# Two decoder layers on eight elements: attention calls in another order, the start regrouped, the routing in smaller steps

## What is computed

```python
# layer 0 (norm before), layer 1 (norm after); ctx is the second input
h = ln1(x); x = x + attn(h, h, causal=True)                # first call  (c = 0)
h = ln2(x); x = x + attn(h, ctx, causal=False)             # second call (c = 1)
h = ln3(x); x = x + relu(h @ w1 + b1) @ w2 + b2            # feed-forward, FFN
x = LN1(x + attn(x, x, causal=True))                       # third call  (c = 2)
x = LN2(x + attn(x, ctx, causal=False))                    # fourth call (c = 3)
x = LN3(x + moe(x))    # router: 2 of 8 experts for each row, gelu, all float32
```

## Time and profile before

| | |
|---|---|
| median of 3 runs | 1236.32 us (1233.37 to 1236.89) |
| profiled execution: its own time, its span | 1233.35 us, 1231.6 us |
| PE, DVE, ACT, POOL busy | 89%, 67%, 59%, 42% of the span |
| mean granted TensorE clock | 0.954 of full speed |
| first `max` matmul of call 0; last `shift` (call 31); first expert matmul | 27.69 us; 844.10 us; 912.42 us |

### The profile page before, as it was taken

How to read it: one execution, slowest core, us unless ns; L and a number is a source line. 1 busy time by engine, 2 the same in 40 slices (tenths; PEclk the granted TensorE clock), 3 DMA queues, 4 the chain that set the end, 5 groups by cost and what they waited for, 6 DMA issues and landing times. The chain is left out here.

```text
span 1231.6 us, 27064 instructions
## 1 busy us (share of the span) xinstructions
PE 1099.5 (89%) x8981; PEld 907.1 (74%) x8981; DVE 821.4 (67%) x2495; ACT 729.9 (59%) x1537; POOL 513.8 (42%) x732
## 2 busy tenths in 40 slices
PE   8688889999999999998899988887879999999960
PEld 7466667768877788876667766555669999999960
DVE  2677878775555555546767777764348888888856
ACT  4345555665555454545566666544338988988842
POOL 4354555331122213434667245442241544544544
PEclk9799999999999999999999999987889999999985
DMA  7575747664344433434746644540656777787764
GB/s 167 90 118 130 120 73 100 84 120 59 43 59 61 52 53 53 87 53 54 160 76 95 88 71 87 95 81 27 228 201 181 250 227 230 240 246 232 237 177 145
DMA packets 110312, 152.35 MB, mean 124 GB/s; under 512 B 23040, under 2 KB 94976, under 8 KB 103424
## 3 DMA queue, kind: packets, MB, share of 16 engines
q1 hardware_dynamic: 101712, 140.21, 51.7%
q0 software_dynamic: 8352, 10.80, 4.5%
q10 hardware_dynamic: 144, 0.02, 0.0%
HBM read 78.39 MB, written 21.62 MB: 81 GB/s over the span
## 5 line engine op out<-in xcount | busy, mean ns | idle before, releaser
L875 ACT ACTIVATE probs<-s 128x384 f32<-128x384 f32 (+1 forms) x512 | 265.5, 541 | 194.4 <-PE s L683 174.3
L946 DVE TENSOR_REDUCE neg_max<-s 128x2 f32<-128x512 f32 x256 | 169.7, 689 | 95.4 <-PE s L658 89.2
L683 PE MATMUL s<-q_stack,k_stack 98*128 98x256 bf16 (+1 forms) x1024 | 176.9, 262 | 14.4 <-ACT probs L875 13.3
L541 POOL TENSOR_SCALAR_AFFINE_SELECT probs<-probs 128x256 f32<-128x256 f32 x256 | 102.3, 409 | 179.7 <-ACT probs L875 179.6
L943 DVE CUSTOM_DVE_ANT_0 s<-s,mask_qk 128x256 f32<-128x256 f32 x256 | 114.2, 446 | 86.0 <-PE s L655 78.0
L683 PEld LDWEIGHTS s<-q_stack,k_stack 98*128 98x128 bf16 x1024 | 90.7, 99 | 40.2 <-ACT probs L875 24.6
L702 PE MATMUL pv<-probs,v 128*32 128x256 f32 (+1 forms) x2048 | 116.1, 369 | 4.0 <-POOL probs L541 3.9
L658 PE MATMUL s<-k_stack,q_stack 96*128 96x256 bf16 x512 | 98.2, 276 | 12.8 <-DVE neg_max L946 11.2
L1303 PE MATMUL moe<-rows_hi,e_w_hi 128*128 128x256 f32 x368 | 104.8, 285 | 3.7 <-DVE rows_lo L1414 2.3
L1303 PE MATMUL moe<-e_w_hi,e_hidden_hi 128*128 128x256 f32 x368 | 104.6, 284 | 0.0
L604 PE MATMUL work<-hT,w_qk 128*128 128x256 f32 x384 | 94.9, 391 | 10.8 <-ACTq L797 10.8
(11 more groups left out here) (195 smaller groups left out, 2651.4 us busy)
## 6 DMA issues: line engine op xcount, KB each, us to landing
w<-in_expert_w SPq DMA_DIRECT2D x26, 1024.0 KB, 5.2
k_stack<-k_part SPq DMA_DIRECT2D x192, 128.0 KB, 4.3
q_stack<-q_part SPq DMA_DIRECT2D x192, 128.0 KB
e_w<-in_expert_w SPq DMA_DIRECT2D x24, 1024.0 KB
rows<-slots_x SPq DMA_DIRECT2D x25, 256.0 KB
slots_x<-filler SPq DMA_DIRECT2D x8, 518.0 KB
cT<-in_context SPq DMA_DIRECT2D x16, 256.0 KB, 4.5
e_b<-in_expert_b SPq DMA_DIRECT2D x24, 128.0 KB
```

Of the source, the lines that this page charges most:

```text
L541: pool.affine_select(out=blocks, in_=blocks, compare_op=ALU.is_ge, fill=0.0, base=0, pattern=[[0, TILES], [1, P]], channel_multiplier=-1). ...
L683: last = pe.matmul(dst[:, kt * S:kt * S + S - q0], k[:, kt * P:(kt + 1) * P], q[:, q0:S], start=True, stop=True)
L875: act.activation(probs[hd][:, 0:width], s2[hd % 2][:, 0:width], ACT.Exp, scale=SCALE).then_inc(probs_ready, 1)
L946: dve.tensor_reduce(neg_max[:, :, hd], src[:].rearrange("p (t s) -> p t s", t=TILES), AX_X, ALU.max, negate=True).then_inc(s1_free, 1)
```

## The change

The calls get a new order: `CALL_OF_SLOT` names the call of each of the 32 slots, lanes in order within each kind. Slots 0 to 7 are the eight first calls and 8 to 14 seven second ones, as before; then come third call 0, second call 7, third calls 1 to 3, fourth 0, third 4, fourth 1, third 5 and 6, fourth 2, third 7, fourth 3 to 7. All that was numbered `c * B + lane` is numbered by slot. The weights of q and k for the third and fourth calls are loaded as soon as the last projection that used their buffer is done, those of v and o as before.

Beside it: (1) call 1 has its norm, `T`, `k`, `q` and `v` ahead of the maxima of call 0, the unused transposes come behind its `v` and are 40 instead of 80, and for calls 0 and 1 ACT, not SP, issues the six DMAs of `q_stack`. (2) DVE's `choose` ends after the maxima of the logits, and the rest of it is a step `pick`; `give_slots` ends where the ranks' bank is free, and the rest is a step `place`. (3) Some due times move by 0.1 to 1.3 units. ACT's copy of the transposed rows (`T`) comes one exponential earlier in each beat, DVE's `wo` one head later, POOL's `bias` one mask earlier, ACT's `scale` of a final norm one exponential later.

```diff
-LAG = {"scalar": {"T": 0.1, "q": 1.4, "k": 1.7, "v": 2.0, "out_T": 0.1, "up": 1.4, "head": 0.6, "shift": 0.5, "final_T": 0.5, "out": 1.4, "scale": 2.4},
-       "vector": {"max": 0.6, "q": 2.2, "k": 1.9, "shift": 2.8, "wo": 1.6, "down": 0.4, "turn": 0.7, "ln": 0, "apply": 3.6, "router": 0.6, "rank": 1.0},
-       "gpsimd": {"mask": 0.6, "bias": 0.2, "ln": 0, "gain": 3.3, "q": 3.7, "k": 2.9, "scatter": 0},
-       "sync": {"q": 5.2, "k": 5.8, "shift": 0.5, "store": 0.2, "fetch": 0.3, "context": 0.1}}
-AT = {"shares": (68.5, 71.5, 74.0, 77.0), "fill": 79.0, "ln": -7.4, "T": -1.9, "q": 0.4, "k": -0.9, "v": 6.4, "bias": 11.7, "context": 8.3, "max": 14.8, "shift": 28.3, "head": 32.8, "weigh0": 43.7,
-      "weigh1": 50.0, "turn": 52.5, "out_T": 55.0, "wo": 56.5, "ffn_ln": 59.5, "ffn_T": 62.7, "ffn_bias": 67.4, "up": (68.0, 73.3, 75.1, 76.7),
-      "down": (79.0, 81.5), "final_ln": 59.3, "final_T": 64.7, "store": 63.1, "router": 65.5, "rank": 67.7, "scatter": 85.5, "post_ln": -15.3}
+LAG = {"scalar": {"T": 0, "q": 1.4, "k": 1.7, "v": 1.9, "out_T": 0.1, "up": 1.4, "head": 0.6, "shift": 0.5, "final_T": 0.5, "out": 1.4, "scale": 2.4},
+       "vector": {"max": 0.5, "q": 2.2, "k": 1.9, "shift": 2.8, "wo": 1.6, "down": 0.4, "turn": 0.7, "ln": 0, "apply": 3.6, "router": 0.6, "rank": 1.0, "pick": 0.6,
+                  "place": 0.6},
+       "gpsimd": {"mask": 0.6, "bias": 0.2, "ln": 0, "gain": 3.4, "q": 3.7, "k": 2.9, "scatter": 0},
+       "sync": {"q": 5.2, "k": 5.8, "shift": 0.5, "store": 0.3, "fetch": 2.8, "context": 0}}
+AT = {"later": 0.0, "pick": 65.9, "place": 68.60000000000001, "shares": (68.5, 71.5, 74.0, 77.0), "fill": 79.0, "ln": -7.5, "T": -1.9, "q": 0.4, "k": -0.8,
+      "v": 6.4, "bias": 10.4, "context": 8.3, "max": 14.8, "shift": 28.3, "head": 32.8, "weigh0": 43.7, "weigh1": 50.0, "turn": 52.5, "out_T": 55.0,
+      "wo": 56.5, "ffn_ln": 59.5, "ffn_T": 62.8, "ffn_bias": 67.4, "up": (68.0, 73.3, 75.1, 76.7), "down": (79.0, 81.5), "final_ln": 59.9, "final_T": 64.7,
+      "store": 63.1, "router": 65.5, "rank": 67.8, "scatter": 85.5, "post_ln": -15.3}
+SECOND = {"ln": -3.0, "T": 1.0, "q": 8.0, "k": 7.0, "v": 9.0}
+ACT_STACKS = 2
+CALL_OF_SLOT = "00000000111111121222323223233333"
+ORDER = [(int(c), CALL_OF_SLOT[:n].count(c)) for n, c in enumerate(CALL_OF_SLOT)]
 def plan_call(n):
-    c, lane = divmod(n, B)
+    c, lane = ORDER[n]
...
+    if n == 1:
+        steps = [(SECOND["ln" if kind == "apply" else kind] - SLOT if kind in SECOND or kind == "apply" else at, kind, lane, arg) for at, kind, lane, arg in steps]
...
                 else:
-                    _, c = what
-                    if c >= 2:
-                        sp.wait_ge(work_full, filled("wo", B - 1, c - 2))
-                    load_qk(c)
-                    load_vo(c)
+                    part, c = what
+                    if part in ("w", "qk"):
+                        if c >= 2:
+                            sp.wait_ge(work_full, max(filled("q", B - 1, c - 2), filled("k", B - 1, c - 2)))
+                        load_qk(c)
+                    if part in ("w", "vo"):
+                        if c >= 2:
+                            sp.wait_ge(work_full, filled("wo", B - 1, c - 2))
+                        load_vo(c)
...
             def stack_q(lane, c):
-                n = c * B + lane
+                n = CALL[c, lane]
+                if n < ACT_STACKS:
+                    return
...
-                if lane == 0 and c == 0:
-                    idle(2 * WARM)
+                if lane == 1 and c == 0:
+                    idle(WARM)
...
                     last.then_inc(ready, 1)
+                    if kind == "q" and n < ACT_STACKS:
+                        stack_q(n)
                 return step
+            def stack_q(n):
+                for i in range(PARTS):
+                    act.wait_ge(q_part_ready[i], n + 1)
+                    for block, p in enumerate(Q_PART_OF_ROWS):
+                        if p == i:
+                            act.dma_start(q_stack[n][block * DK:(block + 1) * DK], q_part[i][:]).then_inc(q_stacked[n], 16)
...
                 for i in range(TILES):
                     dve.max(ordered[:, i, :], logits[:, i, :])
+
+            def pick(lane, stage):
                 dve.drain()
+                ordered = top[:]
...
                 dve.sem_inc(freed("rank", lane, stage), 1)
+
+            def place(lane, stage):
                 dve.tensor_tensor(slot_chosen[:], chosen[:], slot_e[:].unsqueeze(1).to_broadcast([P, TOP, TILES, E]), ALU.mult)
```

More of the change, by code:

```diff
@@ L89, in plan_call @@
         steps += plan_norm(AT["post_ln" if c in POST else "ln"], lane, c)
-    if not CAUSAL[c] and c // 2 * B + lane + CONTEXTS < 2 * B:
+    if not CAUSAL[c] and CONTEXT[c, lane] + CONTEXTS < 2 * B:
         steps += [(AT["context"], "context", lane, c)]
@@ L97, in plan_call @@
     if c == 1:
-        steps += plan_norm(AT["ffn_ln"], lane, FFN) + [(AT["ffn_T"], "T", lane, FFN), (AT["ffn_bias"], "bias", lane, FFN)]
-        steps += [(at, kind, lane, j) for kind in ("up", "down") for j, at in enumerate(AT[kind])]
+        later = FFN_LATER[lane]
+        steps += plan_norm(AT["ffn_ln"] + later, lane, FFN) + [(AT["ffn_T"] + later, "T", lane, FFN), (AT["ffn_bias"] + later, "bias", lane, FFN)]
+        steps += [(at + later, kind, lane, j) for kind in ("up", "down") for j, at in enumerate(AT[kind])]
@@ L100, in plan_call @@
     elif c == CALLS - 1:
-        steps += plan_norm(AT["final_ln"], lane, FINAL) + [(AT[kind], kind, lane, FINAL) for kind in ("final_T", "store", "router", "rank", "scatter")]
-        steps += [(at, "share", lane, i) for i, at in enumerate(AT["shares"])]
+        steps += plan_norm(AT["final_ln"], lane, FINAL) + [(AT["store"], "store", lane, FINAL)]
+        later = AT["later"] * (B - 1 - lane)
+        steps += [(AT[kind] + later, kind, lane, FINAL) for kind in ("final_T", "router", "pick", "rank", "place", "scatter")]
@@ L103, in plan_call @@
+        steps += [(at + later, "share", lane, i) for i, at in enumerate(AT["shares"])]
         if lane in (B - 3, B - 2):
-            steps += [(AT["fill"], "fill", lane, FINAL)]
+            steps += [(AT["fill"] + later, "fill", lane, FINAL)]
+    if n == 1:
+        steps = [(SECOND["ln" if kind == "apply" else kind] - SLOT if kind in SECOND or kind == "apply" else at, kind, lane, arg) for at, kind, lane, arg in steps]
     return [(n * SLOT + at, kind, lane, arg) for at, kind, lane, arg in steps]
@@ L108, in plan_fetches, with at @@
 def plan_fetches():
+    def at(c, lane):
+        return SLOT * CALL[c, lane]
     steps = [(1.5, "fetch", 0, "rows")]
[L111 to L113 removed]
+    steps += [(at(0, lane) - SLOT * 3 + 3.0, "fetch", lane, "x") for lane in range(3, B)]
@@ new lines, in plan_fetches @@
+    steps += [(at(1, 0) - SLOT * FETCH["w"] + 2.0, "fetch", 0, ("w", 1)), (at(1, 0) - SLOT * FETCH["ffn"] + 2.0, "fetch", 0, "ffn"),
+              (at(1, 0) - SLOT * FETCH["contexts"] + 2.0, "fetch", 0, "contexts"), (at(1, 0) - SLOT + 2.0, "fetch", 0, "router")]
+    steps += [(at(c - 2, B - 1) + after, "fetch", 0, (what, c)) for c in (2, 3) for what, after in (("qk", FETCH["qk"]), ("vo", FETCH["vo"]))]
+    steps += [(at(1, B - 1) + SLOT * FETCH["expert"] + max(FFN_LATER[B - 1], 0), "fetch", 0, "expert")]
@@ L346, in run, with norm_before @@
                 step[kind](lane, arg)
+        def norm_before(lane, stage):
+            same = [(other, s) for _, kind, other, s in STEPS if kind == "ln" and use(s) == use(stage)]
+            at = same.index((lane, stage))
+            return same[at - 1] if at and by_three(*same[at - 1]) else None
         def wait_norm(engine, lane, stage):
@@ L897, in norm @@
                 k = use(stage)
-                if lane > 0 and by_three(lane - 1, stage):
-                    dve.wait_ge(rstd_ready, nth("ln", lane - 1, stage))
+                other = norm_before(lane, stage)
+                if other:
+                    dve.wait_ge(rstd_ready, nth("ln", *other))
                 for i in range(TILES):
@@ L1073, in _ @@
             run({"ln": others(norm), "apply": others(apply_norm), "q": rest("q", q_part[0], q_rest, bq, q_part_ready[0], q_rest_ready), "k": rest("k", k_part[0], k_rest, bk, k_part_ready[0], k_rest_ready),
-                 "max": row_max, "shift": rest_of_shift, "turn": normalise, "wo": attended, "down": fed_forward, "router": choose, "rank": give_slots, "share": share}, LAG["vector"])
+                 "max": row_max, "shift": rest_of_shift, "turn": normalise, "wo": attended, "down": fed_forward, "router": choose, "pick": pick, "rank": give_slots, "place": place, "share": share}, LAG["vector"])
             tiles_of_experts()
```

54 lines of the change are left out of this document (31 added, 23 removed).

## The result

The changed kernel takes 1226.77 us (median of 6 runs, 1225.24 to 1227.65), the kernel before 1233.48 (6 runs on the same chip, 1230.85 to 1236.89): a ratio of 0.995, 95% interval 0.9931 to 0.9969. It is faster, by 7 us where 20 were forecast.

What follows compares the result with a forecast made beforehand. PE, busy 89% of the span, was taken as the bound. Terms 0 - 13 - 3 - 4 + 0 = -20 gave 1213 us from the profiled 1233.35 and 1216 from the median 1236.32; predicted 1215, range 1201 to 1230.

Steps and rivals of the forecast that it cites:

- The order of calls, 0: Mixing third and fourth calls among second and third adds no PE work and gains 0 us, ends -6 and +6.
- The final beats, -13: Five `shift`-to-`shift` windows with final steps: routing cut in two on DVE frees PE's waits, 137.55 to 124.5 us.
- second payment: After PE's wait for a maximum in final beats, slow matmuls at low clock cost 1.65 us or more again.
- Rival B: DVE's rank, `turn` and `place` block is only moved; final beats keep most of their 27 us: -9, 1226 us; chance 0.17.
- The start, -4: Call 0's maxima run without call 1's work among them; its `shift` comes near 43.1 instead of 47.04 us: -4.
- ACT's copy one exponential earlier, -3: PE's projections wait less for ACT's copy of T, about 0.4 us in each of nine causal beats: -3 us.
- POOL jamming (C): Beats 21 to 26: causal masks wait on POOL behind gains or scatter, stopping PE; +10, 1245 us; chance 0.05.
- a paying mixture (A): All parts work, final beats fall to PE's work and causal beats give their room: -32, 1203 us; chance 0.17.
- The first expert matmul: Sign in the changed profile that the forecast is right: the first expert matmul comes near 892 us.

Runs made afterwards that it cites:

- the start alone: Kernel before, old order, with only the new start (call 1 early, ACT issuing q stacks, 40 unused transposes, other fetch lags): 1228.12 us, ratio 0.996.
- the changed kernel's second profile: Profile from the control group that ran the changed kernel again unaltered: 1227.3 us (12 runs), ratio 0.9971.
- the last set: Second set of the changed kernel with place, final_T, router and pick later: 1224.4 us; the same without the new start: 1225.17 us.
- the first experiment: Changed kernel with the calls in the order of before, new start, due times and smaller routing steps kept: 1225.01 us, ratio 0.9936.
- the small steps alone: Kernel before, old order, with only the routing cut in two (pick with rank behind maximum 7, place behind turn): 1228.5 us, ratio 0.9979.

## Why the forecast was half right

*The order of calls, 0: right,* shown by three pairs of kernels that differ in nothing else (-2, -2 and -4.5 us for the old order, none beyond its interval). All three have the small steps; beside the routing in one piece the new order has no such pair, and there it seems to cost some 5 us (1.0 with it, 0.996 for the start alone with the old one, two kernels that differ in some due times too). That it adds no PE work held. What the forecast missed is that two things about cancel in it: in the three pairs of profiles the finals are 5 to 7 us shorter among causal calls, and FFN and plain beats are 6 to 11 us longer. Two of these costs were seen: the 1.69 us for `h_ffn`, and beat 28, a plain beat of 23.44 us, in which the last lane's norm lies on DVE (PE waits 1.83 us for a maximum at 774.37).

*The final beats, -13: this is the step that failed;* it measured -4.77. Of the miss of 13.5 us (forecast -20, measured -6.50), 8.2 lie in the final beats, 5.0 in FFN and plain beats (2.17 + 2.85), 0.5 in what comes ahead of beat 11 (the start and ACT's copy), and 0.3 go the other way behind them. The -4.77 is not the mechanism of the forecast either: PE's idle time in these beats, which was to fall, went from 19.15 to 19.21 us. The step that failed is the wait that the sum put at nothing with the words "PE next asks for maximum 8, which is behind rank, `turn` and `place`, but PE has `v` (1.7 us) to do first". The block lasts 3.6 us, so 1.7 us of `v` cover half of it. The forecast had both numbers, gave the block its own rival at 0.17, and still did not set one against the other in its sum. In beats 22, 24, 27 and 29 PE waits 1.58, 1.57, 1.42 and 0.61 us for maxima, 5.2 in all. That place is what made the block too long is shown by the run that moves it alone: these waits go, and 4.4 us of the four beats with them, against the changed kernel's second profile.

*Waits that weren't named.* The final transposes on PE wait 4.2 us for POOL's gain in the same four beats. POOL now does that gain beside the masks of a causal call, which fourth calls don't have. The forecast named the gain for what it does to masks and to DVE's cast, and not for PE's transposes behind it. At full clock there is the wait for the split's bank as well (0.95 and 1.39 us in beats 22 and 24). With these waits the four beats are 8.2 us longer than forecast. The forecast also counted the slow matmuls behind a wait as a second payment; in beats 22 and 24 they were hardly one, as the two profiles show (26.24 and 26.59 us at a low clock, 26.27 and 26.09 at full clock). Moving the transposes makes the wait for the gain smaller; its price in time is not shown apart from the clock.

*Rival B* has the right mechanism, a block of DVE that is only moved, and its 1226 in part by luck: the final beats gave 4.8 us, not the 2 that it allowed them, and the 5.0 us that FFN and plain beats took back are not in it.

*The start, -4: right,* 43.41 us against 43.1, and -0.4% for the start alone. Over all profiles the `shift` of call 0 lies at 43.3 to 45.1 us with the new start and at 46.3 to 49.5 with the old one; that all of it reaches the end is shown for the start alone, and not in the last set, where the two kernels differ by 0.8 us. The reasoning behind it held as well: the first maximum came at 30.49 us where 30.5 was worked out, and the next came without a gap. Timeline of DVE:

```profile
30.49 0.43 DVE L998 CUSTOM_DVE_ANT_0 s<-s,mask_qk 128x256 f32<-128x256 f32 x1 [0.26 <-issue]
...
43.41 0.41 DVE L1008 TENSOR_TENSOR neg_max_T<-work,neg_max_T 16x256 bf16<-16x256 f32 x1 [0.26 <-ACT neg_max_T L884]
```

*ACT's copy one exponential earlier, -3: right in size.* Each of beats 1 to 5 is 0.38 us shorter, for which 0.4 was taken, 1.90 in all. Beats 19 to 21, which project third calls, show the same where the order is the old one: 20.99, 20.84 and 21.47 us in the first experiment against 21.36, 21.23 and 21.84 before, 1.1 in all. Beat 0 gave nothing. With the start alone or the small steps alone, which have the old due time of the copy, four of beats 1 to 5 or all of them keep their length of before; no run moves the copy by itself. Beat 9 is 0.83 us shorter; what shortens it was not followed.

*POOL jamming (C) and a paying mixture (A)* are refuted: plain mixed beats take 21.03 to 21.45 us, and PE waits for masks 1.5 us in two places from beat 22 on.

*The first expert matmul* was to be near 892 us and came at 904.63. That is the same miss, 8.2 us in the final beats and 5.0 in the plain and FFN ones.

## What to carry to other kernels

A wait that is cut by moving work behind the next item of a queue is only gone if that work, added up instruction by instruction with its stretched lengths, is shorter than what the waiting engine has to do meanwhile: put the two sums beside each other (3.6 against 1.7 us here) before putting the wait at nothing. Look at what a step holds besides time: `rank` could not be late because `v` needs its bank, `place` holds nothing that PE wants and could be moved freely, and that one due time was worth 4 to 7 us. When an order is changed, follow each engine's helper steps (gains, last norms) to their new neighbours, not the big ones alone.

## What the runs showed that was not expected

A small cast on DVE ends when POOL's vector instruction beside it ends. In beat 24 of the changed kernel the cast takes from 682.91 to 683.86, and POOL's timeline has

```profile
682.66 1.18 POOL L540 TENSOR_TENSOR x<-x,row 128x512 f32<-128x512 f32 x1
```

which ends at 683.84. In beats 22 and 27 the casts (0.78 and 0.77 us) end at 635.50 and 752.45, POOL's instructions beside them at 635.47 and 752.43. In the kernel with place and transposes later and the old order one took 1.65 us, from 742.13 to 743.78, beside an instruction of POOL that ends at 743.75. (That one started 0.43 us behind the cast, while a scatter's DMA was being issued; why the cast had not gone ahead is open.) Where nothing ran on POOL it took 0.17 us. By the Trainium skill (SBUF — State Buffer, section Who interferes with whom) the two engines share a port pair that one holds for a whole instruction; the trace agrees, with ends 0.02 to 0.03 us apart.

One kernel's median can differ by 0.6% between two sets of six runs (1215.04 and 1224.4 us), while each set's interval says 0.26%. The clock differed, and so did the chip. A difference below that needs both kernels in one set, and then again.
